# Cross attention on Trainium2: the value products of two chunks of keys in one visit, in slots 0 to 41 of three batches

## What is computed

```
q = x @ Wq.T + bq                      # 512 tokens
k, v = split(c @ Wkv.T + bkv)          # 1601 rows of context
q, k = rms_norm(q, q_gamma), rms_norm(k, k_gamma)
scores = einsum("bhnd,bhmd->bhnm", q, k) / sqrt(16)
out = einsum("bhnm,bhmd->bhnd", softmax(scores), v)
```

## Time and profile before

| what | value |
| --- | --- |
| median of 3 launches | 1329.47 us (1328.87 to 1329.97) |
| the profiled launch, its own time | 1329.02 us |
| its span | 1327.2 us |
| PE, PEld | 1187.1 us (89%), 732.2 us (55%) |
| ACT | 903.4 us (68%) |
| POOL | 703.4 us (53%) |
| DVE | 670.4 us (51%) |

### The profile page before, as it was taken

The page is one execution under the profiler, slowest core; times in us unless marked ns, Lnnn a source line. Parts: engine busy times, 40 slices in busy tenths (PEclk is TensorE's granted clock), DMA queues, the critical chain, the costliest instruction groups (busy, mean ns, idle before and its releaser), DMA issues.

```text
span 1327.2 us, 27690 instructions
## 1 busy us (share of the span) xinstructions
PE 1187.1 (89%) x8670; PEld 732.2 (55%) x8670; DVE 670.4 (51%) x2202; ACT 903.4 (68%) x1821; POOL 703.4 (53%) x810
## 2 busy tenths in 40 slices
PE   5999999999999885899999999999999889999960
PEld 4666776776776564433333333433222479889950
DVE  6676567557655557563135413542554353333328
ACT  4656546546655425668976897689989669789950
POOL 1776557657656612355217521753277757766640
PEclk9999999999999998999999999999999999999985
DMA  7998665445546621100001000000274576665559
GB/s 235 354 326 285 224 212 193 170 153 189 180 139 202 205 64 34 34 19 17 18 26 42 18 17 25 27 21 16 68 274 150 188 251 196 209 199 176 178 170 380
DMA packets 146755, 195.05 MB, mean 147 GB/s; under 512 B 12048, under 2 KB 132512, under 8 KB 145968
## 3 DMA queue, kind: packets, MB, share of 16 engines
q1 hardware_dynamic: 135856, 162.97, 38.1%
q0 software_dynamic: 10752, 30.26, 6.3%
HBM read 71.01 MB, written 122.18 MB: 146 GB/s over the span
## 4 chain that ended last, share of the span: by engine, by line
PE 56%; ACT 17%; issue 9%; DVE 8%; DMA 5%; POOL 3%; SPq 1%; ACTq 1%; POOLq 0%; DVEq 0%
ACT xa_probs L1404 9%; PE sa_pf L354 9%; PE xa_banks L1243 7%; PE xa_banks L1258 6%; PE sa_po L436 5%; PE xa_banks L1126 5%; PE mo_banks L2115 5%; PE sa_pf L387 4%; PE sa_ps L411 4%; PE sa_ptr L422 4%; ACT sa_probs L478 2%; PE mo_banks L2124 2%; DMA mo_w_all<-in_down_p 1%; PE mo_banks L2103 1%; DMA mo_w_all<-slots 1%
## 5 line engine op out<-in xcount | busy, mean ns | idle before, releaser
L1404 ACT ACTIVATE xa_probs<-xa_banks 128x1024 f32<-128x1024 f32 (+1 forms) x416 | 401.9, 1045 | 83.7 <-PE xa_banks L1243 82.7
L341 POOL TENSOR_SCALAR sa_probs<-sa_probs,sa_recip 128x128 f32<-128x128 f32 (+3 forms) x256 | 275.2, 1087 | 169.4 <-DVE sa_recip L598 168.9
L478 ACT ACTIVATE sa_probs<-sa_probs,sa_neg_max 128x128 f32<-128x128 f32 (+3 forms) x256 | 141.8, 555 | 154.4 <-DVE sa_neg_max L535 154.4
L1258 PE MATMUL xa_banks<-xa_probs,xa_v_one 128*17 128x512 f32 (+1 forms) x1664 | 218.7, 598 | 6.9 <-ACT xa_q_aug L1350 4.6
L1243 PE MATMUL xa_banks<-xa_q_aug,xa_k_aug 32*128 32x512 f32 (+1 forms) x1664 | 153.1, 441 | 13.7 <-issue 3.7
L2031 POOL DMA_INDIRECT slots<-mo_y,mo_dest x128 | 122.8, 960 | 59.4 <-issue 45.3
L2115 PE MATMUL mo_banks<-mo_xs_t,mo_gu 128*128 128x128 f32 x1024 | 136.3, 276 | 0.0
L2115 PEld LDWEIGHTS mo_banks<-mo_xs_t,mo_gu 128*128 128x128 f32 x1024 | 125.6, 193 | 0.1
L535 DVE CUSTOM_DVE_ANT_0 sa_probs<-sa_ps,sa_toeplitz 128x128 f32<-128x128 f32 (+3 forms) x256 | 115.1, 486 | 14.2 <-PE sa_ps L411 12.9
L1243 PEld LDWEIGHTS xa_banks<-xa_q_aug,xa_k_aug 32*128 32x128 f32 (+1 forms) x1664 | 61.3, 179 | 106.7 <-ACT xa_probs L1404 74.7
L422 PE MATMUL sa_ptr<-sa_ident,sa_probs 128*128 128x128 f32 x640 | 95.4, 275 | 9.7 <-ACT sa_pt L501 7.6
(11 more groups left out here) (321 smaller groups left out, 2268.4 us busy)
## 6 DMA issues: line engine op xcount, KB each, us to landing
rows<-sa_blank SPq DMA_DIRECT2D x128, 548.0 KB, 4.3
mo_xs<-rows SPq DMA_DIRECT2D x128, 137.0 KB
slots<-sa_blank SPq DMA_DIRECT2D x48, 256.0 KB, 6.2
mo_w_all<-slots SPq DMA_DIRECT2D x24, 512.0 KB, 13.1
xa_raw<-in_ctx_t SPq DMA_DIRECT2D x24, 256.0 KB, 2.8
mo_w_all<-in_gate_up_p SPq DMA_DIRECT2D x2, 2816.0 KB, 15.6
sa_toeplitz<-extended_bias SPq DMA_DIRECT2D x8, 512.0 KB, 7.8
mo_w_all<-in_down_p SPq DMA_DIRECT2D x2, 2048.0 KB, 17.0
```

The source lines that it names most:

```text
L341: pool.tensor_scalar(probs[:, t % SLOTS, 0:w], probs[:, t % SLOTS, 0:w], recip[:, col:col + 1], None, ALU.mult).then_inc(probs_ready, 1)
L478: act.activation(probs[:, t % SLOTS, 0:w], probs[:, t % SLOTS, 0:w], ACT.Exp, bias=neg_max[:, i:i + 1], scale=-1.0, accum_out=sums[:, i:i ...
L1258: last = pe.matmul(banks[32 * i:32 * i + XD + 1, 6 + group % 2, :], v_one[b % 2][0:m, c, 4 * g + i, :], probs[0:m, (2 * j + i // 2) % RING ...
L1404: act.activation(probs[0:m, n % RING, :, :], banks[0:m, 2 * (n % 3):2 * (n % 3) + 2, :], ACT.Exp).then_inc(probs_ready, 1)
```

## The change

In batches 0, 1 and 2, slots 0 to 41 (`PAIRED` = 42), the values are made in even slots only, two chunks at a time: slot s takes the chunks of slots s - 2 and s - 1. An odd slot has none. In an even slot the step of `PLAN` now comes ahead of the values. The exceptions are slots in which one of the two chunks begins a group (slots 2, 14, 28 and 40): there, as in every slot that is not paired, the values come first and the step last. The number of the group that decides the bank of a step, and the wait for `o_ready`, follow the new order. DVE copies a group that has ended in the slot in which its last chunk is now made, ahead of the slot's own copy where two chunks of two groups meet. What each instruction computes stays as it was.

```diff
+    PAIRED = 42
...
+    def values_of(b, s):
+        j = b * SLOTS + s
+        if b < 0:
+            return []
+        if b < B - 1 and s < PAIRED:
+            chunks = [j - 2, j - 1] if s % 2 == 0 else []
+        else:
+            chunks = [j - LAG_PV]
+        return [v for v in chunks if 0 <= v < B * SLOTS]
+
+    def values_first(b, s):
+        return not (0 <= b < B - 1 and s < PAIRED) or any(v % KT == 0 for v in values_of(b, s))
...
-                group = (b * SLOTS + s - LAG_PV) // KT
-                if group >= 1:
-                    pe.wait_ge(o_ready, group)
+                copied = (b * SLOTS + s) // KT if kind == "o" else group_at[f]
+                if copied >= 1:
+                    pe.wait_ge(o_ready, copied)
...
                     if 0 <= b < B:
                         scores(j, shifted)
-                    if 0 <= j - LAG_PV < B * SLOTS:
-                        times_v(j - LAG_PV)
-                    prepare(b, s)
+                    if not values_first(b, s):
+                        prepare(b, s)
+                    for v in values_of(b, s):
+                        times_v(v)
+                    if values_first(b, s):
+                        prepare(b, s)
...
                 for s in slots_of(b):
+                    crossing = len(values_of(b, s)) == 2 and values_first(b, s)
+                    if crossing:
+                        copy_groups(b, s)
                     evacuate(b, s)
                     if b < 0:
                         low_first(s)
-                    j = b * SLOTS + s - LAG_PV
-                    if j >= 0 and j % KT == KT - 1:
-                        group = j // KT
-                        dve.wait_ge(pv_done, j + 1)
-                        dve.tensor_copy(o_sb[:], banks[:, 6 + group % 2, :]
-                                        ).then_inc(o_ready, 1)
+                    if not crossing:
+                        copy_groups(b, s)
```

More of the change, by code:

```diff
@@ L719, in step_of @@
         return step
+    def values_of(b, s):
[9 more added lines that the diff above has]
+        return not (0 <= b < B - 1 and s < PAIRED) or any(v % KT == 0 for v in values_of(b, s))
     fill_at, bank_at, left_by, holder = {}, {}, {}, {}
+    group_at = {}
     act_out, dve_out, prepared, before = {}, {}, {}, {}
     n_act = n_dve = 0
-    for b in range(-1, B + 1):
-        for s in slots_of(b):
-            group = (b * SLOTS + s - LAG_PV) // KT
[L727 to L730, removed]
+    group = -1
+    for b, s, part in ((b, s, part) for b in range(-1, B + 1) for s in slots_of(b) for part in range(2)):
+        if (part == 0) == values_first(b, s):
+            for v in values_of(b, s):
+                if v % KT == 0:
+                    group = v // KT
+                    left_by[group] = holder.get(6 + group % 2)
+        elif step_of(b, s) is not None:
             kind = step_of(b, s)[0]
             f = len(fill_at)
+            group_at[f] = group
             bank = PRO_BANKS[f % 8] if b < 0 else 7 - group % 2
@@ L742, in cross_attention, with copies_o @@
                 prepared[b + 1] = f
+    def copies_o(b, s):
+        return [v // KT for v in values_of(b, s) if v % KT == KT - 1]
     def fill_of(batch, kind, i):
@@ L1614, in evacuate, with copy_groups @@
                                           ).then_inc(x2_part, 1)
+            def copy_groups(b, s):
+                for group in copies_o(b, s):
+                    dve.wait_ge(pv_done, (group + 1) * KT)
+                    dve.tensor_copy(o_sb[:], banks[:, 6 + group % 2, :]).then_inc(o_ready, 1)
             def normalise_x(batch):
```

## The result

The changed kernel took 1362.09 us (median of 4, 1361.12 to 1364.63) against 1329.17 for the kernel before in the same session: a ratio of 1.0248, 95% interval 1.0232 to 1.0265. It is slower by 33 us; 1360 was forecast.

A forecast was written before the change was run, and what follows sets the result against it. PE was taken to set the pace, with ACT as full in slots 26 to 39 of batch 1. Five parts gave +9.3 us, with 1.0 coming back 10.3 for batch 1; three batches +31, so 1329 + 31 = 1360, range 1350 to 1369.

The forecast's parts named there:

- The merged visit: Two chunks of values in one PE visit take 1.84 us instead of 1.96, a gain of 0.12 a pair.
- The gate: In odd slots the next scores wait until ACT's first exponential has read their banks, 1.85 us a slot.
- The wait behind ACT's copy: Even slots' step starts 1.42 us behind the scores, as ACT copies after both exponentials; 0.75 of empty PE.
- The wait behind DVE's copy: Even slots' step after "kv" or "q" starts 1.00 us behind the scores instead of 0.67, 0.33 more.
- part 1: Batch 1, pairs 26 to 38, where ACT copies: 5.69 us each, 39.8 against 32.21 now, +7.6.
- Part 2: Batch 1, pairs 4, 16, 24 at 5.27 us against 4.46 and pair 10 at 6.29 against 5.10: +3.6.
- Part 3: Batch 1, pairs 0, 2, 8, 20, 22 with two heavy steps: 34.6 us against 33.4, +1.1.
- Part 4: Batch 1, pairs 6 and 40 without wait for a copy: 5.36 and 4.94 us against 5.48 and 5.32, -0.5.
- Part 5: Batch 1, pairs 12, 14, 18: 17.4 us against 19.9, -2.5, of which 1.0 was taken to come back through DVE.
- only the gate counts: Rival: copies are hidden and only uneven slots remain; +1.0 us a batch, 1332 us; chance 0.07.
- the merge is all that counts: Rival: only the 0.12 us saved a pair is left; -7.6 us, 1321.5 us; chance 0.04.
- DVE late everywhere: Rival: 2.5 us return in pairs 12, 14, 18, plus late "kv" copies in slots 6 to 8; 1366 us; chance 0.20.

The follow-up runs named there:

- e2: Changed kernel with ACT's copy of a kt or qt step in odd paired slots moved between the slot's two exponentials; 1344.28 us, 1.0109 of the kernel before.
- e5: e2 with the first exponential of odd paired slots cut to 512 of its 1024 columns; 1337.47 us, 1.0080 of the kernel before.
- e6: Changed kernel with DVE's second copy of a "kv" step cut from 16 heads to one; 1357.36 us, 1.0224 of the kernel before.
- e10: e8 with the value visit merged in pair 0 of batches 0 to 2 alone; 1321.96 us, 0.9951 of the kernel before.
- e1: Changed kernel with the values ahead of the step in every even slot; 1355.27 us, 1.0197 of the kernel before.
- e8: Kernel before with DVE's last query norms part moved to slot 14 and second key norms' last two parts one slot later; 1322.74 us, ratio 0.9957.
- e3: Kernel before with visits merged only in pairs 0, 2, 8, 20 and 22 of each batch; 1329.29 us, 1.0010 of the kernel before.
- e9: Changed kernel with the same move of DVE's norms as e8; 1358.23 us, 1.0230 of the kernel before.

## Why the prediction was right

The measured 1362.1 lies in the range of 1350 to 1369, 2 us above the forecast of 1360, and the likeliest case is the one that came. Its mechanism is shown by e2, e5 and e6, which take away the wait for ACT's copy, a part of the gate and a part of the wait for DVE's copy, one after the other, and find the pairs where the pieces put them. The closeness of the total is in part luck: misses of 0.2 us and more in single pairs cancel, as the list shows. By the steps of the prediction:

- **The merged visit**: 1.84 us forecast, 1.84 measured (782.80 to 784.64). Here the Trainium skill's rule of the drain at a change of tiling mode (TensorEngine Tiling (Array Packing), Key Properties) and the trace agree; no run parts the drain from other costs of the turn between two kinds of work. The merge gains 0.16 us where nothing stands against it, in pair 0 of batches 1 and 2 (e10).
- **The gate**: 1.85 in odd slots, as forecast (784.64 to 786.49), and e5 moved it by the length of one exponential.
- **The wait behind ACT's copy**: 1.42 behind the scores forecast, 1.41 measured; e1 and e2 take it away in two ways and find 4.95 and 4.93 us for the pair, where 4.94 was priced.
- **The wait behind DVE's copy**: 1.00 forecast; 0.93 to 1.00 measured behind "kv", but 1.38 in slot 8 of batch 0; e6 takes 0.25 of it away. Behind "q", where 1.00 was taken without a row, the step of slot 10 starts at 0.87: pair 10 took 6.15 where 6.29 was forecast.
- **The sum for batch 1**: part 1 39.8 forecast, 41.4 measured, 39.8 without the fall of the clock in it (so in batches 0 and 2). Two misses cancel in it: pair 28, in which a group begins, took 5.88 instead of 5.69, and pair 38 took 5.48, since ACT's copy ahead of its step is of the last chunk, with 65 keys, and takes 0.40 us instead of 0.60. Part 2, 22.1 forecast, 21.9 measured. Part 3, 34.6 and 34.3. Part 4, 10.3 and 10.5: slot 40 does wait 0.2 us, for DVE's copy of the group. Part 5, 17.4 and an allowance of 1.0, and 18.2.
- **What the sum lacked.** In the profiled launch, 1.6 us in pair 38 of batch 1 (the clock) and 2.6 in pair 14 of batch 2 (1.15 of wait, 1.42 of clock). Without these three terms the paired stretches grew by 10.3, 9.8 and 10.7, 30.9 in all against the 31 of the forecast. Slots 42 to 51 grew by 0.5 in batches 0 and 1: ACT's copy for slot 41 (810.89) stands ahead of the first exponential of slot 42 (811.37, 1.23 behind its scores in place of 0.77), and slot 42 has no step, so it is at the gate. That 1.0 and the 2.6 of pair 14 are more than the difference between +31 and the +33 of the medians.
- **Part 5** was right in its cause, DVE's norms (e8), and in saying that they would cost again where PE comes earlier: pair 14 did so in e1 (8.93) and e5 (7.24). Its allowance of 1.0 was a guess between two bounds: 0.7 came back in batches 0 and 1 and 3.3 in batch 2. That the wait of pair 14 in batch 2 was longer (DVE's chain starts 1.1 us later there, since POOL squares the queries later) and was followed by a fall of the clock was not foreseen.
- **The range.** Its low end is added up wrongly: part 1 with a wait of 0.5 (1.75 less) and nothing of part 5 back (1.0 less) gives 10.3 - 2.75 a batch, about +23 and not +24. The range itself, rounded down to +21, holds.

The rival "only the gate counts" took all copies as hidden. e2 hides ACT's alone, and took 1344 where the rival was priced at 1332. Its light pairs came out at the 4.94 that the rival priced; the other 12 us lie in the waits behind "kv" (1.75 us a batch by e6), in pairs 12 to 18, in pair 40 of batch 2 and in slots 42 to 51. The rival "the merge is all that counts" is excluded by the result itself, and for the five pairs that suit it best by e3. The rival "DVE late everywhere" (0.20) came true in part: in batch 2 part 5 gave back more than its 2.5, and slot 8 of batch 0 has the late "kv" copy that it named; in the rest slots 6 to 8 came as forecast (pair 6 5.35 against 5.36).

## What to carry to other kernels

Before two visits are merged, ask what ran beside the one that moves away. Here each value visit was the cover for the copy of the last step out of the only bank and for the turn through ACT; with the cover gone, 0.12 us of saved switching bought waits of 0.3 to 0.75 us in even slots and a 1.85 us floor in odd ones. And where an engine serves a tight loop and a slack one in one program, the place of a single instruction can be worth more than its length: moving one ACT copy by one instruction gave back 18 us, and moving some of DVE's norms by one slot made the kernel before 0.4% faster.

## What was not expected of the hardware

- TensorE's granted clock fell to 1.2 GHz for 3.4 us at a time in the middle of stretches where PE was busy for 86 to 87% on the whole. Behind the wait of slot 14 of batch 2 it did so in all five profiles that have the wait (the change, e1, e2, e5, e6); in a light pair it did so once. Slot 15 took 3.78 us in place of 2.36, so the fall cost about as much as the wait ahead of it.
- In slots 34 to 41 of the kernel before, where ACT works without a gap, the recorded length of its exponentials climbs from one to the next, to 1.24 us in slot 37 and again to 1.21 in slot 41 (1.02 in most other rows), the same in batches 0, 1 and 2, though the two of a slot start 0.90 us apart all the same. The length of such a row is no measure of the work in it; the distance between starts is.
- DVE's small instructions of 128x64 took 0.22 to 0.23 us each in slot 14 of the changed kernel, but 1.32 and 0.78 us in the same chain a little before. The long ones end with work of POOL:

```profile
725.80 1.27 POOL L994 TENSOR_TENSOR xa_ct_lo<-xa_raw,xa_ct_hi 128x512 fp32r<-128x512 f32 x1
725.83 1.32 DVE L1464 TENSOR_TENSOR xa_rms_tmp<-xa_rms_tmp,xa_square_sum 128x64 f32<-128x64 f32 x1
```

  Of the 108 such instructions in the norms of the cross attention (TENSOR_TENSOR and SCALAR_TENSOR_TENSOR), 20 took over 0.35 us in the changed kernel, and each of the 20 ended 0.08 us behind the end of an instruction of POOL; it is so in the kernel before. In e8 and e9 some of them run a slot later, and only 8 are long. No run moved POOL's work, so that POOL holds them up is a reading of these times and not shown.
